# An attention layer with an 8-bit linear branch on one core: the first head's orders and the last head's row groups rearranged

## What is computed

```
xn = layernorm(x)                                  # 1024 x 256
q, k, v = xn @ Wq, xn @ Wk, xn @ Wv                # 16 heads of 128
q, k = rmsnorm(q, q_rms_w), rmsnorm(k, k_rms_w)    # over the 128 of a head
s = q @ k.T / sqrt(128) - slope[h] * (t - s)       # causal, ALiBi bias
y = rmsnorm(softmax(s) @ v, subln_w)               # per head
attention = concat(y) @ Wproj                      # 2048 -> 256
ffn = qdq_fp8(xn) @ (fp8_weight * scale).T         # 256 -> 256
```

## Time and profile before

| | |
|---|---|
| median of 3 runs | 519.19 us (518.9 to 522.19) |
| the profiled execution, its own time | 518.89 us |
| its span | 517.1 us |
| busy: PE, VectorE (DVE), ScalarE (ACT), GpSimd (POOL) | 505.1, 419.6, 379.2, 349.3 us |
| head 0's first score | at 24.1 us |
| head 1's first score | at 50.9 us |
| last matmul, last addition, last store issued | 512.6, 513.2, 514.8 us (starts) |

### The profile page before, as it was taken

How to read it: one execution, slowest core, us unless ns; L and a number is a source line. 1 busy time by engine, 2 the same in 40 slices (tenths; PEclk the granted TensorE clock), 3 DMA queues, 4 the chain that set the end, 5 groups by cost and what they waited for, 6 DMA issues and landing times.

```text
span 517.1 us, 11927 instructions
## 1 busy us (share of the span) xinstructions
PE 505.1 (98%) x3337; PEld 466.9 (90%) x3337; DVE 419.6 (81%) x996; ACT 379.2 (73%) x894; POOL 349.3 (68%) x500
## 2 busy tenths in 40 slices
PE   7998999999999999999999999999999999999996
PEld 4987998999999899999989999999999989999885
DVE  5689789788888987888798888978878898788975
ACT  4878686787867768786776968678786876878562
POOL 6788785857858387783858758585785838758301
PEclk9999999999999999999999999999999999999999
DMA  6101001010010101001010000101001000000002
GB/s 176 53 2 42 1 1 42 3 42 0 2 41 0 41 0 41 0 0 41 0 41 0 14 27 0 41 0 41 0 0 41 0 10 0 10 3 1 1 2 82
DMA packets 18615, 10.84 MB, mean 21 GB/s; under 512 B 2208, under 2 KB 18592, under 8 KB 18592
## 3 DMA queue, kind: packets, MB, share of 16 engines
q1 hardware_dynamic: 17600, 10.49, 6.9%
q10 hardware_dynamic: 992, 0.07, 0.1%
HBM read 9.51 MB, written 1.05 MB: 20 GB/s over the span
## 4 chain that ended last, share of the span: by engine, by line
PE 88%; DVE 5%; ACT 2%; POOL 2%; issue 2%; DMA 1%; DVEq 0%; POOLq 0%
PE pT_ps L702 12%; PE qkv_ps L608 10%; PE qkv_ps L610 9%; PE qkv_ps L609 8%; PE yT_ps L610 7%; PE yT_ps L608 7%; PE yT_ps L609 7%; PE score_big L608 4%; PE score_big L610 4%; PE score_big L609 4%; PE misc L667 2%; PE score_small L609 2%; PE score_small L610 2%; PE score_small L608 2%; PE misc L608 1%
## 5 line engine op out<-in xcount | busy, mean ns | idle before, releaser
L1003 ACT ACTIVATE stage<-qkv_ps 128x384 f32<-128x384 f32 x116 | 57.1, 492 | 85.8 <-PE qkv_ps L610 85.7
L1317 DVE TENSOR_TENSOR pT_lo<-pT_ps,pT_hi 128x384 fp32r<-128x384 f32 (+2 forms) x192 | 100.2, 550 | 10.5 <-ACT pT_hi L1035 10.5
L1035 ACT ACTIVATE pT_hi<-pT_ps 128x384 fp32r<-128x384 f32 (+2 forms) x192 | 86.7, 486 | 26.1 <-PE pT_ps L702 26.0
L1025 ACT ACTIVATE probs<-probs,neg_max 128x384 f32<-128x384 f32 (+7 forms) x128 | 99.2, 776 | 5.0 <-DVE neg_max L1308 4.4
L702 PE MATMUL pT_ps<-ident,probs 128*128 128x128 f32 x576 | 85.9, 276 | 4.1 <-DVE pT_lo L1317 4.0
L608 PE MATMUL qkv_ps<-w_hi,xT_hi 128*128 128x384 f32 x240 | 87.6, 365 | 0.8 <-DVE xT_lo L1397 0.8
L610 PE MATMUL qkv_ps<-w_hi,xT_lo 128*128 128x384 f32 x240 | 81.0, 337 | 0.0
L702 PEld LDWEIGHTS pT_ps<-ident,probs 128*128 128x128 f32 x576 | 66.2, 141 | 16.2 <-ACT probs L1025 5.0
L609 PE MATMUL qkv_ps<-w_lo,xT_hi 128*128 128x384 f32 x240 | 80.6, 336 | 0.0
L608 PE MATMUL yT_ps<-pT_hi,v_hi 128*128 128x256 f32 (+1 forms) x224 | 73.1, 326 | 0.0
L610 PE MATMUL yT_ps<-pT_hi,v_lo 128*128 128x256 f32 (+1 forms) x224 | 72.0, 322 | 0.0
(11 more groups left out here) (214 smaller groups left out, 1298.4 us busy)
## 6 DMA issues: line engine op xcount, KB each, us to landing
w_raw<-in_wq SPq DMA_DIRECT2D x16, 128.0 KB, 2.2
w_raw<-in_wk SPq DMA_DIRECT2D x16, 128.0 KB, 2.3
w_raw<-in_wv SPq DMA_DIRECT2D x16, 128.0 KB, 2.3
wp_raw<-in_wproj SPq DMA_DIRECT2D x16, 128.0 KB, 2.1
acc<-in_x SPq DMA_DIRECT2D x4, 256.0 KB, 4.8
out<-acc SPq DMA_DIRECT2D x8, 128.0 KB, 2.0
w<-in_ffn_w ACTq DMA_DIRECT2D x1, 64.0 KB, 5.4
q_col<-in_q_w ACTq DMA_DIRECT2D x1, 0.5 KB, 3.0
```

What stands on the lines that cost most here:

```text
L1003: act.activation(stage_of(h, k // 2)[:, k % 2, :], qkv_bank(h, k)[:, 0:3 * D], ACT.Copy).then_inc(qkv_read, 1)
L1025: act.activation(probs[:, s % 2, 0:(i + 1) * P], probs[:, s % 2, 0:(i + 1) * P], ACT.Exp, bias=neg_max[:, par, s:s + 1], scale=-1.0, accum ...
L1035: act.activation(pT_hi[g][:, a:b, r * P:(r + 1) * P], pT_ps[(chunk0(h, s) + k) % 2][:, 0:(b - a) * P].rearrange("p (j t) -> p j t", t=P), ...
L1317: dve.tensor_tensor(pT_lo[g][:, a:b, r * P:(r + 1) * P], pT_ps[(chunk0(h, s) + k) % 2][:, 0:(b - a) * P].rearrange("p (j t) -> p j t", t=P ...
```

## The change

Three things are done. The lists of the start and of head 0 are put in another order on PE, ScalarE, VectorE and GpSimd. The lists of the last head are put in another order on PE, ScalarE and VectorE. And the last head's second group, row tiles 5, 4, 1, 0, is attended, summed and projected in two pairs, 5 and 4, then 1 and 0, where it was three tiles and one; so its output jobs are two instead of three, and a wait for the square is added ahead of the subtraction (`lo_last`). No operation on the data is otherwise added or taken out. The diff (the context cut; a line "..." where lines are left out):

```diff
@@ -35,7 +35,7 @@
     LAST_GROUPS = [[7, 6, 3, 2], [5, 4, 1, 0]]
-    LAST_PARTS = [(0, 0, 4), (1, 0, 3), (1, 3, 4)]
+    LAST_PARTS = [(0, 0, 4), (1, 0, 2), (1, 2, 4)]
     LAST_SMALL = [i for i in LAST_ORDER if i < 4]
@@ -67,7 +67,7 @@
     LAST_BANK = {"proj0a": None, "proj0b": "qkv", "proj1a": "qkv", "proj1b": None}
-    LAST_JOBS = [(0, 0, 2, "big0"), (0, 2, 4, "big1"), (1, 0, 2, "big0"), (1, 2, 3, "big1"), (1, 3, 4, None)]
+    LAST_JOBS = [(0, 0, 2, "big0"), (0, 2, 4, "big1"), (1, 0, 2, "big0"), (1, 2, 4, "big1")]
     MISC_FIRST = [m for m in MISC if m.startswith("qkT")]
@@ -320,7 +320,7 @@
-    return score_small[:, 0:P] if p == 2 else yT_ps[:, 0:(LAST_PARTS[p][2] - LAST_PARTS[p][1]) * P]
+    return score_small[:, 0:2 * P] if p == 2 else yT_ps[:, 0:(LAST_PARTS[p][2] - LAST_PARTS[p][1]) * P]
@@ -521,10 +521,10 @@
     norm_qk(0, 0)
+    split_v(0, 0, 0)
     norm_qk(0, 1)
...
     norm_qk(0, 3)
-    split_v(0, 0, 0)
     split_v(0, 0, 1)
@@ -539,8 +539,8 @@
         norm_qk(1, 3)
+        split_wp(0, 0)
         split_v(1, 1, 1)
-        split_wp(0, 0)
         split_v(1, 1, 2)
@@ -757,7 +757,7 @@
         g, a, b, bank = LAST_JOBS[n]
-        pe.wait_ge(y_split, 2 * (H - 1) + (n // 2 + 1 if n < 4 else 3))
+        pe.wait_ge(y_split, 2 * (H - 1) + max(1, n))
         if n == 0:
@@ -816,29 +816,29 @@
+    transpose_x(0)
     warm(2)
+    transpose_x(1)
     warm(2)
-    transpose_x(0)
-    transpose_x(1)
     project(0, 0, 0)
     project(0, 0, 1)
+    transpose_x(2)
     project(0, 0, 2)
-    transpose_x(2)
+    project(0, 0, 3)
     transpose_x(3)
-    project(0, 0, 3)
     project(0, 0, 4)
...
     transpose_qk(0, 0, 0, -1)
+    project(1, 1, 1)
     transpose_qk(0, 0, 1, -1)
-    project(1, 1, 1)
     transpose_qk(0, 0, 2, -1)
+    project(1, 1, 2)
     score(0, 0, 0)
-    project(1, 1, 2)
     transpose_qk(0, 0, 3, -1)
-    transpose_probs(0, 0)
+    project(1, 1, 3)
@@ -851,33 +851,33 @@
     def first_head():
-        project(1, 1, 3)
         project(1, 1, 4)
...
         score(0, 0, 2)
+        transpose_probs(0, 0)
         project(1, 1, 5)
         project(1, 1, 6)
+        transpose_probs(0, 1)
         score(0, 0, 3)
-        transpose_probs(0, 1)
+        score(0, 0, 4)
         project(1, 1, 7)
-        score(0, 0, 4)
         transpose_probs(0, 2)
+        transpose_probs(0, 3)
+        score(0, 0, 5)
         transpose_qk(1, 1, 0, 0)
-        score(0, 0, 5)
-        transpose_probs(0, 3)
+        transpose_qk(1, 1, 1, 0)
         score(0, 0, 6)
-        transpose_qk(1, 1, 1, 0)
         transpose_probs(0, 4)
         score(0, 0, 7)
+        transpose_qk(1, 1, 2, 0)
         transpose_probs(0, 5)
-        transpose_qk(1, 1, 2, 0)
         attend(0, 0, 0, 0)
+        transpose_qk(1, 1, 3, 0)
         transpose_probs(0, 6)
-        transpose_qk(1, 1, 3, 0)
         attend(0, 0, 0, 1)
+        score(1, 1, 0)
         transpose_probs(0, 7)
         transpose_w8()
-        score(1, 1, 0)
@@ -955,35 +955,34 @@
         sum_y(H - 2, 0)
+        transpose_probs(H - 1, 1)
         score(H - 1, 1, 2)
         project_out(H - 2, 0, 0, 0, H - 1)
+        project_out(H - 2, 0, 0, 1, H - 1)
         score(H - 1, 1, 3)
-        transpose_probs(H - 1, 1)
-        project_out(H - 2, 0, 0, 1, H - 1)
+        sum_y(H - 2, 1)
         score(H - 1, 1, 4)
         transpose_probs(H - 1, 2)
-        sum_y(H - 2, 1)
         project_out(H - 2, 0, 1, 0, H - 1)
...
         attend_last(0)
+        score(H - 1, 1, 6)
         transpose_probs(H - 1, 5)
-        score(H - 1, 1, 6)
+        sum_last(0)
         score(H - 1, 1, 7)
-        sum_last(0)
+        project_last(0)
         transpose_probs(H - 1, 6)
         transpose_probs(H - 1, 7)
-        project_last(0)
         attend_last(1)
-        project_last(1)
         attend_last(2)
         sum_last(1)
+        project_last(1)
         sum_last(2)
...
         project_last(3)
-        project_last(4)
@@ -1081,65 +1080,65 @@
     round_w()
+    round_xT(0)
     normed(1)
-    round_xT(0)
     round_xT(1)
     act.wait_ge(const_ready, 3)
+    make_bias(0, 0)
     copy_qkv(0, 0)
-    make_bias(0, 0)
     copy_qkv(0, 1)
+    square_qk(0, 0)
+    round_xT(2)
     copy_qkv(0, 2)
-    round_xT(2)
+    copy_qkv(0, 3)
     round_xT(3)
-    square_qk(0, 0)
-    copy_qkv(0, 3)
     square_qk(0, 1)
...
     copy_qkv(0, 5)
+    square_qk(0, 2)
     copy_qkv(0, 6)
-    square_qk(0, 2)
     copy_qkv(0, 7)
...
     act.wait_ge(wq_col_ready, 1)
+    copy_qkv(1, 0)
     qk_hi(0, 0, 0)
-    copy_qkv(1, 0)
+    copy_qkv(1, 1)
+    square_qk(1, 0)
     qk_hi(0, 0, 1)
     qk_hi(0, 0, 2)
-    copy_qkv(1, 1)
-    exps(0, 0, 0)
     copy_qkv(1, 2)
     qk_hi(0, 0, 3)
-    probs_hi(0, 0)
-    square_qk(1, 0)
+    exps(0, 0, 0)
     copy_qkv(1, 3)
+    copy_qkv(1, 4)
...
     def first_head():
-        copy_qkv(1, 4)
         square_qk(1, 1)
+        probs_hi(0, 0)
         exps(0, 0, 1)
+        probs_hi(0, 1)
         copy_qkv(1, 5)
+        copy_qkv(1, 6)
         square_qk(1, 2)
-        probs_hi(0, 1)
-        copy_qkv(1, 6)
+        exps(0, 0, 2)
+        exps(0, 0, 3)
+        probs_hi(0, 2)
         copy_qkv(1, 7)
-        exps(0, 0, 2)
+        probs_hi(0, 3)
+        exps(0, 0, 4)
         square_qk(1, 3)
-        probs_hi(0, 2)
-        exps(0, 0, 3)
-        probs_hi(0, 3)
         qk_hi(1, 1, 0)
-        exps(0, 0, 4)
+        qk_hi(1, 1, 1)
+        probs_hi(0, 4)
         exps(0, 0, 5)
-        probs_hi(0, 4)
+        exps(0, 0, 6)
         probs_hi(0, 5)
-        exps(0, 0, 6)
-        qk_hi(1, 1, 1)
         qk_hi(1, 1, 2)
+        qk_hi(1, 1, 3)
+        probs_hi(0, 6)
+        exps(0, 0, 7)
         make_bias(1, 1)
-        probs_hi(0, 6)
-        qk_hi(1, 1, 3)
-        exps(0, 0, 7)
         act.wait_ge(wb_ready, 1)
@@ -1233,11 +1232,11 @@
         exps(H - 1, 1, 0)
+        exps(H - 1, 1, 1)
         probs_hi(H - 1, 0)
-        exps(H - 1, 1, 1)
         square_y(H - 2, 1)
+        probs_hi(H - 1, 1)
         y_hi(H - 2, 0, 1)
-        probs_hi(H - 1, 1)
         exps(H - 1, 1, 2)
@@ -1246,19 +1245,19 @@
         square_last(0)
+        hi_last(0)
+        el2_last(0)
         probs_hi(H - 1, 5)
-        hi_last(0)
         exps(H - 1, 1, 6)
...
         probs_hi(H - 1, 6)
-        el2_last(0)
         probs_hi(H - 1, 7)
...
         square_last(1)
+        el2_last(2)
         hi_last(1)
-        el2_last(2)
+        square_last(2)
         hi_last(2)
-        square_last(2)
@@ -1460,37 +1459,37 @@
-    quarter_tables()
     moments(0)
...
     moments(1)
+    spread(1)
     shift_x(0)
-    spread(1)
     shift_x(1)
+    quarter_tables()
     moments(2)
     split_xT(0)
+    moments(3)
     spread(2)
-    moments(3)
     spread(3)
...
     normed(3)
+    mean_squares(0, 0)
     split_xT(2)
     split_xT(3)
-    mean_squares(0, 0)
+    norm_first(0)
     mean_squares(0, 1)
-    norm_first(0)
     mean_squares(0, 2)
...
     qk_lo(0, 0, 0)
-    mask(0, 0, 0)
+    mean_squares(1, 0)
     qk_lo(0, 0, 1)
     qk_lo(0, 0, 2)
+    mask(0, 0, 0)
+    decode_w8(0)
     qk_lo(0, 0, 3)
-    probs_lo(0, 0)
-    mean_squares(1, 0)
@@ -1501,34 +1500,34 @@
     def first_head():
-        decode_w8(0)
         decode_w8(1)
...
         mean_squares(1, 1)
-        mean_squares(1, 2)
         decode_w8(3)
+        probs_lo(0, 0)
+        decode_w8(4)
+        probs_lo(0, 1)
         mask(0, 0, 3)
-        probs_lo(0, 1)
+        decode_w8(5)
         mask(0, 0, 4)
         probs_lo(0, 2)
-        decode_w8(4)
+        decode_w8(6)
+        mean_squares(1, 2)
+        probs_lo(0, 3)
+        mask(0, 0, 5)
         mean_squares(1, 3)
-        decode_w8(5)
-        mask(0, 0, 5)
-        probs_lo(0, 3)
-        decode_w8(6)
         qk_lo(1, 1, 0)
...
         mask(0, 0, 6)
+        qk_lo(1, 1, 1)
+        mask(0, 0, 7)
+        probs_lo(0, 5)
+        qk_lo(1, 1, 2)
+        qk_lo(1, 1, 3)
+        probs_lo(0, 6)
         decode_w8(7)
-        probs_lo(0, 5)
-        qk_lo(1, 1, 1)
-        qk_lo(1, 1, 2)
-        mask(0, 0, 7)
-        probs_lo(0, 6)
-        qk_lo(1, 1, 3)
         scale_ffn()
@@ -1601,6 +1600,7 @@
         dve.wait_ge(y_hi_done, 2 * (H - 1) + p + 1)
+        dve.wait_ge(y_squared, 2 * (H - 1) + p + 1)
         dve.tensor_tensor(yT_lo[:, g, at], last_yT(p), yT_hi[:, g, at].bitcast(f32),
@@ -1616,7 +1616,7 @@
         dve.wait_ge(proj_ready, 4 * (H - 1) + n + 1)
-        dve.wait_ge(y_normed, 2 * (H - 1) + (n // 2 + 1 if n < 4 else 3))
+        dve.wait_ge(y_normed, 2 * (H - 1) + max(1, n))
         for r in range(a, b):
@@ -1625,41 +1625,40 @@
         mask(H - 1, 1, 1)
+        part_y(H - 2, 0)
         add_out(H - 3, 1, 1)
-        part_y(H - 2, 0)
         probs_lo(H - 1, 0)
...
         mask(H - 1, 1, 2)
-        y_lo(H - 2, 1)
         add_out(H - 2, 0, 0)
         probs_lo(H - 1, 1)
+        y_lo(H - 2, 1)
+        mask(H - 1, 1, 3)
         add_out(H - 2, 0, 1)
         y_mean(H - 2, 0, 1)
-        mask(H - 1, 1, 3)
         mask(H - 1, 1, 4)
...
```

(11 more changed lines are left out.)

## The result

On one chip, turn about with the kernel before, the changed kernel took **517.11 us** (median of 14 executions, 516.31 to 519.5) against 520.48 (14, 518.9 to 522.73): ratio 0.9934, 95% interval 0.9921 to 0.9948, so 2.7 to 4.1 us less. I had forecast 516.9 and no change beyond 1%. The profiled execution took 516.31 (span 514.4), against 518.89 (span 517.1): 2.6 us less, where I had summed 2.3. The medians differ by more, 3.4 us, and the kernel before has a median of 520.48 here where the forecast started from 519.19, its first three executions.

The account below looks back on a forecast made before the run. PE, busy 98% of the span, was taken as the bound, so only its stalls could give time. From the profiled 518.89: less 1.8 (head 0), 0 (start, last head) and 0.5 (end) is 516.6, forecast 516.9; range 515.2 to 519.8.

Parts of the forecast that it names:

- PE's stalls in head 0: Head 0: five PE stalls, 3.8 us in all, with VectorE as releaser; the upper bound on gains from new orders there.
- my sign of being wrong: Head 0: forecast wrong if VectorE's busy share from 36 to 48 us stays at 98% with PE's stalls as before.
- my walk: Head 0: hand walk of the new orders with profiled durations; stalls 3.8 us before, 1.85 after, so 2.0 gained.
- Head 0: 1.8 forecast: Head 0: new orders cut PE's stalls; 2.0 us, taken as 1.8, lasting to the end.
- Start: 0 forecast: Start: new orders move the first projection from 10.98 to 11.2; booked 0, between +0.4 and −0.3 us.
- Last head up to tile 2: 0 forecast: Last head up to probs_lo(15,2): same VectorE operations in another order, gain 0; 0.9 us more if the cover went.
- The two new stalls: Last head: PE waits 0.45 before sum_y(14,1) and 0.4 before project_out(14,1,0), paid out of 0.94 us already lost at 496.44.
- End: 0.5 forecast: Kernel end: last addition at 513.3 instead of 513.68, stores done at 514.7 instead of 515.22; 0.5 us, between 0 and 1.0.
- a last store issued near 514.7: Kernel end: a sign expected in the profile after, the last output store issued near 514.7 us.
- The waits only move: Head 0 rival: exponentials come 0.7 us later than walked, PE waits as before, only the store end is won: 518.7; chance 0.23.
- The late decode: Head 0 rival: decode_w8(7), moved later, delays the attend of group 1 by 0.7 us: 519.9; chance 0.12.
- The clock of the warm-up: Start rival: thinned warm-up lets PE's clock fall, 4.6 us to return, half lost: 519.2; chance 0.05.

Follow-up runs that it names:

- e5: Kernel before with the rest of the last head's new orders but its old parts, without the pairs: 520.43 us, ratio 0.9994.
- e7: Changed kernel with decode_w8(7) moved forward on VectorE, right behind the mask of row tile 6 of head 0: 517.41 us, ratio 0.9939.
- e11: Changed kernel with 16 warm-up matmuls, all ahead of the first transposes, and the last head's tile 7 score ahead of tile 5's transposes: 517.48 us, ratio 0.9942.
- e10: Changed kernel with all 20 warm-up matmuls ahead of the first transposes and the last head's tile 7 score ahead of tile 5's transposes: 516.48 us, ratio 0.9924.
- e4: Kernel before with only head 0's new orders on all engines, start and last head as they were: 519.1 us, ratio 0.9965.

## Why the prediction was right

**The number, and luck in it.** The sum is of the profiled execution, and there it holds: 2.3 us forecast, 2.6 measured. That 516.9 lies only 0.2 from the median of 517.11 is luck. The median of before came out 1.3 higher than the 519.19 that I started from, and the gain between the medians is 3.4, 1.1 more than forecast; the two misses cancel.

**What bounds it.** PE's stalls in head 0, as read: PE's named waits there fell from 3.0 (2.6 for `pT_lo`, 0.4 for `kT_lo`) to 0.9, and the lead won there reached the end whole. VectorE did not get free, though: its share from 36 to 48 us is 98% as before, the first half of my sign of being wrong, and only the second half, PE's stalls, changed. Of the 1.5 us that VectorE stood for the squares 0.78 came back as a wait for `pT_hi` that my walk had not. So I read the gain as one of the order in which a full VectorE serves PE, more than of its free time. That is argued, not shown: of the single moves in head 0 only that of the decode was tried by itself.

**Head 0: 1.8 forecast, 1.64 measured** at the first transposes of head 1, 1.75 at the last head. The walk's marks against the trace: first score 28.2 / 28.18; tile 6's transposes 37.15 / 37.45, wait 0.8 / 0.75 for the exponentials; tile 3's 40.55 / 41.06; tile 5's 42.8 / 43.26, wait 0.4 / 0.15; `transpose_qk(1,1,3)` 45.15 / 45.55; attend of group 1 51.35 / 51.75; head 1's transposes 53.75 / 54.17. The walk runs 0.3 to 0.5 early from tile 6 on and the order of events is right. One size in it was off, and luckily so: the decode began at 48.17, 0.6 later than walked, but took 0.68 and not 1.18, and so ended at 48.85, where I had 48.75. ScalarE's `square_y` began at 49.05; a decode of 1.18 would have ended at 49.35, so up to 0.3 of the 1.64 (an estimate from these rows) hangs on it.

**Start: 0 forecast, within 0.1 by the projections** (11.2 / 11.11), 0.2 with the wait between them that I had seen going and booked at nothing. The medians say more than that, and that rest stays open.

**Last head up to tile 2: 0 forecast, 0.1 measured.** The two new stalls came as written (0.45 / 0.42 and 0.4 / 0.21), and the 0.94 fell to 0.34 to pay for them.

**End: 0.5 forecast, 1.0 measured**, the one mis-sized term. Of it the additions are right: 0.38 forecast, 0.31 measured, and the attend of part 1 stands at 506.24 when the lead of 1.75 is added back (506.25 forecast). The stores are not: I gave them 0.1 and they gave 0.67, as I read the 2.29 us of the last four stores as a queue of four, when it was one issue of 0.95 with two behind it. The old parts alone do not bring that issue, since e5 has them without it; what does stays open. One sign was written wrong: "a last store issued near 514.7" leaves out the 1.8 of head 0. With it that is 512.9, and the last issue of the changed kernel ends at 512.59.

I also priced orders and pairs apart from each other. By one profile each they are one term: the orders without the pairs lose 0.58.

**Rivals.** "The waits only move" (0.23): the releaser did change, from `pT_lo` to `probs`, and two new waits came in the last head, but 4.4 us of named waits in both heads became 2.3. "The late decode" (0.12): e7 shows that the late place costs nothing and by the profile wins a microsecond. "The clock of the warm-up" (0.05): 16 matmuls ahead of the first transposes brought the full clock before the projections (products of 384 columns in 0.34 us from 10.8 on in e11, which has no more than those 16), and no profile lost it between the gaps of the start. The Trainium skill's rule that I weighed there (TensorE: Matmul & The Clock Gate, Part 1) holds as to the rise. Against thinning the warm-up nothing shows in the start itself; whether e11's lower mean clock comes from it, six executions cannot say.

## What to carry over

Where the bounding engine stands still for another one, write down which operation of the releaser is early for no one and walk it to the last place that its own reader allows; here that was one decode, worth 1 us by the profiles, with no work changed. An order and a grouping can need each other, so price them together and try them apart. At the end of a kernel look at single issues of the store queue before calling the queue long: with one slow issue among eight the end came 0.6 to 1.2 us later behind the last addition than in e5, which has the same parts.

## What the runs showed of the hardware

- The same decode step (`wb`, 512 columns) took 1.18 us at 44.76 before and 1.04 in e7, each time begun behind a GpSimd operation already running, and 0.68 in the changed kernel, where it began 0.02 ahead of GpSimd's `v_lo`; that one then took 1.26 instead of its usual 0.73. The 0.4 to 0.5 us falls on whichever of the two comes second. The Trainium skill (SBUF — State Buffer, SBUF: two separate sides) says that a VectorE operation with two SBUF inputs and a GpSimd operation that reads SBUF share a port pair, that the one that starts first holds it for its whole instruction, and that the other blocks. This decode has two SBUF inputs, and the rows agree in kind: the second one took 0.50, 0.36 and 0.53 longer where 0.64, 0.50 and 0.66 of the first one were still to run. GpSimd's operation ahead of the decode before, in e7, and then behind it in the changed kernel, one fence each:

```profile
44.67 0.73 POOL L478 TENSOR_TENSOR v_lo<-early_room,v_hi 128x256 fp32r<-128x256 f32 x1
```

```profile
43.20 1.04 POOL L258 TENSOR_TENSOR qk_n<-stage,qk_r 128x512 f32<-128x512 f32 x1
```

```profile
48.19 1.26 POOL L478 TENSOR_TENSOR v_lo<-stage,v_hi 128x256 fp32r<-128x256 f32 x1
...
49.94 0.73 POOL L478 TENSOR_TENSOR v_lo<-stage,v_hi 128x256 fp32r<-128x256 f32 x1
```

- One DMA issue on SP among the eight last stores takes 0.95 to 1.58 us instead of 0.43 in five of thirteen profiles; in e10 it was the second of them (1.42) and cost 0.1 at most (2.84 from the last addition to the end), as six came behind it with time to spare. What makes it long stays open.

```profile
507.61 1.42 SPq L384 DMA_DIRECT2D out<-acc  x1
```

- The granted clock can fall to half within a kernel that keeps PE busy 98% of the time, for 3.4 us, 1.6 us behind a 0.45 us stall (e4), and come back while PE is busy without a gap. Behind the same stall of 0.45 us the kernel before stays at 1.00 (505.80 to 509.50). What makes the difference stays open.
